# The order of a step's work on TensorE in the attention stage of a fused cross-attention and feed-forward layer, with ScalarE and VectorE made to follow it

## The reference

```python
q = Wq @ layernorm(x) + bq ; k = Wk @ ctx + bk ; v = Wv @ ctx + bv   # per batch, 128x128 @ 128x1024
k, v = pad(k, 8 left, 7 right), pad(v, ...)
dots[h, t, w] = sum_d q[h, d, t] * k[h, d, t + w] * hd ** -0.5
attn = softmax(dots, axis=w)
out[h, d, t] = sum_w attn[h, t, w] * v[h, d, t + w]
x = x + tanh(g_xattn) * (Wo @ out + bo)
x = x + tanh(g_ffn) * ((silu(n @ gate) * (n @ up)) @ down)            # n = layernorm(x)
```

## Time and profile before

| | |
|---|---|
| median of 3 runs | 1725.99 us (1715.70 to 1726.87) |
| the profiled execution | 1736.66 us, its span 1734.8 us |
| PE busy | 1607.8 us, 93% of the span, granted clock 0.96 of full speed in the mean |
| VectorE, ScalarE, GpSimd busy | 1516.9, 995.8, 1455.0 us |
| attention, batches 1 to 14 | 394.04 us (52.88 to 446.92), granted clock 0.91 |

### The profile page before, as it was taken

The page is one execution under the profiler, slowest core; times in us unless marked ns, Lnnn a source line. Parts: engine busy times, 40 slices in busy tenths (PEclk is TensorE's granted clock), DMA queues, the critical chain, the costliest instruction groups (busy, mean ns, idle before and its releaser), DMA issues.

```text
span 1734.8 us, 40469 instructions
## 1 busy us (share of the span) xinstructions
PE 1607.8 (93%) x16614; PEld 823.8 (47%) x16614; DVE 1516.9 (87%) x1482; ACT 995.8 (57%) x1134; POOL 1455.0 (84%) x892
## 2 busy tenths in 40 slices
PE   6888889889658999999999999999999999999996
PEld 4565656566533444444444444444444444444444
DVE  4567667667539999999999999999999999999996
ACT  3566667666534555555555555555555555555552
POOL 4556646565647999999999999999999999999975
PEclk8899989899869999999999999999999999999998
DMA  5645645565333222222222222222222222222127
GB/s 120 154 110 150 140 120 132 128 137 126 96 97 97 74 74 73 73 79 79 75 73 73 75 81 76 73 73 73 74 80 78 73 74 74 78 78 76 37 97 291
DMA packets 162354, 166.66 MB, mean 96 GB/s; under 512 B 11918, under 2 KB 127310, under 8 KB 162154
## 3 DMA queue, kind: packets, MB, share of 16 engines
q1 hardware_dynamic: 161018, 163.74, 33.7%
q10 hardware_dynamic: 1152, 0.33, 0.1%
HBM read 113.92 MB, written 16.78 MB: 75 GB/s over the span
## 4 chain that ended last, share of the span: by engine, by line
PE 81%; issue 6%; POOL 5%; ACT 3%; DMA 1%; DVE 1%; SPq 1%; ACTq 0%; POOLq 0%; DVEq 0%
PE bank L1136 63%; PE bank L1043 3%; POOL oacc L564 3%; PE bank L1032 2%; PE bank L999 2%; PE bank L1075 2%; PE bank L1006 2%; PE bank L991 2%; ACT pT L632 2%; PE bank L1053 1%; ACT xn L639 1%; PE bank L1022 1%; PE bank L995 1%; PE bank L1003 1%; PE bank L1011 1%
## 5 line engine op out<-in xcount | busy, mean ns | idle before, releaser
L924 DVE SCALAR_TENSOR_TENSOR acc<-bank,scale,acc 128x1024 f32<-128x1024 f32 x784 | 949.3, 1271 | 17.7 <-PE bank L1136 10.3
L1136 PE MATMUL bank<-xT,w_int 128*128 128x512 f16 x3584 | 851.3, 381 | 12.0 <-ACT acc L733 4.3
L564 POOL TENSOR_TENSOR oacc<-oacc,d_part 128x1024 f32<-128x1024 f32 x336 | 795.0, 2366 | 26.5 <-ACT d_part L753 10.3
L753 ACT ACTIVATE d_part<-bank,scale 128x1024 f32<-128x1024 f32 x336 | 373.5, 1112 | 390.7 <-PE bank L1136 376.8
L1136 PEld LDWEIGHTS bank<-xT,w_int 128*128 128x128 f16 x3584 | 350.5, 98 | 439.4 <-DVE acc L924 7.1
L1136 PE MATMUL bank<-h_hi,d_int 128*128 128x512 f16 x896 | 340.2, 380 | 7.2 <-ACT d_part L753 3.0
L1136 PE MATMUL bank<-h_lo,d_int 128*128 128x512 f16 x896 | 339.5, 379 | 0.0
L506 POOL TENSOR_TENSOR raw_z<-raw_w,raw_z 128x512 int32<-128x512 int32 x168 | 263.9, 1571 | 29.0 <-DMA raw_z<-in_L_ffn_gate_z_dram 12.2
L632 ACT ACTIVATE pT<-bank 96x1024 f16<-96x1024 f16 x128 | 123.4, 1014 | 61.2 <-PE bank L1043 61.2
L1136 PEld LDWEIGHTS bank<-h_hi,d_int 128*128 128x128 f16 x896 | 87.2, 97 | 150.1 <-DVE acc L924 27.8
L820 DVE TENSOR_REDUCE rmax<-bank 128x16 f32<-128x768 f32 x64 | 60.9, 952 | 104.6 <-PE bank L1032 104.6
(11 more groups left out here) (82 smaller groups left out, 1406.1 us busy)
## 6 DMA issues: line engine op xcount, KB each, us to landing
raw_w<-in_L_ffn_gate_w_dram SPq DMA_DIRECT2D x56, 256.0 KB, 3.0
raw_z<-in_L_ffn_gate_z_dram SPq DMA_DIRECT2D x56, 256.0 KB, 3.7
raw_w<-in_L_ffn_up_w_dram SPq DMA_DIRECT2D x56, 256.0 KB, 3.0
raw_z<-in_L_ffn_up_z_dram SPq DMA_DIRECT2D x56, 256.0 KB, 3.7
raw_w<-in_L_ffn_down_w_dram SPq DMA_DIRECT2D x56, 256.0 KB, 2.7
raw_z<-in_L_ffn_down_z_dram SPq DMA_DIRECT2D x56, 256.0 KB, 3.3
vt<-vn_hl SPq DMA_DIRECT2D x64, 192.0 KB
vt<-vn_hl SPq DMA_DIRECT2D x64, 160.0 KB
```

The source lines that it names most:

```text
L564: nc.gpsimd.tensor_tensor(into, into, part, ALU.add).then_inc(d_added, 1)
L753: nc.scalar.activation(d_part[:, (count(0, x, False) - 1) % 2, :], pair[slot][:, :, :].rearrange("p h r -> p (h r)"), ACT.Copy, scale=scal ...
L924: nc.vector.scalar_tensor_tensor(out=into, in0=pair[u % 4][:, :, :].rearrange("p h r -> p (h r)"), scalar=scale[:, par, i, m, k:k + 1], in ...
L1136: last = nc.tensor.matmul(dst[:, h, :], weights, rows_of(h, part), start=(part == 0), stop=(part == 1))
```

## The change

On PE, two of the three tasks of a step now stand between the scores and the mixing, the third between the mixing and the turning, and none behind the turning. Before, one stood in each place. ScalarE takes the third task before it takes the turned probabilities; VectorE takes the third task in its own step instead of behind the next step's `soften`; and ScalarE's `norm_x(b + 1)` moves from the end of step 0 of batch b to its beginning.

```diff
@@ scalar (ACT)
             for b in range(B):
                 for s in range(S):
                     n = S * b + s
-                    behind_scores, behind_mix, behind_turn = tasks_of(b, s)
-                    for t in behind_scores:
+                    if s == 0 and b + 1 < B:
+                        norm_x(b + 1)
+                    first, second, third = tasks_of(b, s)
+                    for t in first:
                         take_high(*t)
                     exp(n)
-                    for t in behind_mix:
+                    for t in second + third:
                         take_high(*t)
                     if n:
                         take_pT(n - 1)
-                    for t in behind_turn:
-                        take_high(*t)
-                    if s == 0 and b + 1 < B:
-                        norm_x(b + 1)
                     if s == 1 and b >= 2:
                         norm_row(b - 2)
@@ vector (DVE)
                     soften(b, s)
-                    if n:
-                        for t in tasks_of((n - 1) // S, (n - 1) % S)[2]:
-                            take_low(*t)
-                    for t in tasks_of(b, s)[0]:
+                    first, second, third = tasks_of(b, s)
+                    for t in first:
                         take_low(*t)
                     if n >= 2:
                         take_mix(n - 2)
-                    for t in tasks_of(b, s)[1]:
+                    for t in second + third:
                         take_low(*t)
                     if s == 0 and b >= 2:
                         moments_row(b - 2)
@@ vector, behind the loop
             invert_sums(S * B - 3)
             invert_sums(S * B - 2)
-            for t in tasks_of(B - 1, S - 1)[2]:
-                take_low(*t)
             take_mix(S * B - 2)
@@ tensor (PE)
                     scores(b, s)
-                    behind_scores, behind_mix, behind_turn = tasks_of(b, s)
-                    for t in behind_scores:
+                    first, second, third = tasks_of(b, s)
+                    for t in first + second:
                         project(*t)
                     if n >= 2:
                         mix(n - 2)
-                    for t in behind_mix:
+                    for t in third:
                         project(*t)
                     if n == 1:
                         pe.wait_ge(s_kept, 2)
                     if n:
                         turn_probs(n - 1)
-                    for t in behind_turn:
-                        project(*t)
```

## The result

The changed kernel takes 1672.75 us in the median of four runs (1665.99 to 1674.17), the kernel before 1725.11 (1715.70 to 1726.87): a ratio of 0.970, interval 0.966 to 0.974. It is 52 us faster. Forecast were 1702 us and a range of 1687 to 1722: the sign is right, the size is not, and the time lies outside the range on the fast side.

The account below looks back on a forecast made before the run. PE bounds attention: 22.2 us of work in 28.15 a batch, the rest waits and half clock. -21 - 1 + 5 - 4 - 6 = -27 gave 1710, 1699 on the medians' scale; with an allowance 1702 us, range 1687 to 1722.

Parts of the forecast that it names:

- `q` wait removed: Attention batches: PE's 13 waits of the `q` projection for `norm_x` vanish, -14.8 us.
- slow clock that goes with it: Attention batches: PE's slow clock behind four of the longer `q` waits goes too, -6 us.
- new waits for `shifted` and pT: Attention batches: the earlier `norm_x` delays ScalarE and VectorE, so PE waits; +5 us, kept at 2 to 10.
- instruction waits, in the mixings: Mixings of steps 0 and 3: longer instruction packets shorten waits by 0.95 and 0.7 us, seven times each, -11.5 us.
- instruction waits, at the other places: Places where packets get shorter: two of them wait 0.5 us, seven times, +7 us.
- first batch: First batch: one more `q` wait goes and `v` lies before a mixing that waits for a DMA, -1 us.
- last batch: Last batch: earlier emptying of `o(14, 1)` lets SP issue `keep_row(14)` and piece 3's loads 6.1 us earlier, -6 us.
- parts 1 and 3: Earlier `norm_x` in the attention batches, -21, -1 and +5 us; SP's earlier issue in the last batch, -6 us.
- Rival A: Attention batches: instruction delivery takes the `q` wait's place; 1716 us, bounds 1709 to 1722, chance 0.30 shared with another rival.
- Rival B: Attention batches: four shortened packets of every eleven wait and drop the clock; slower, 1750 us, chance 0.09.
- part 2: PE's new task order in the attention batches: same work, instruction waits moved by packet density; -4 us taken.
- Rival C: Attention batches: the stalls in the mixing mostly vanish and nothing new appears; 1684 us, chance 0.11.

Follow-up runs that it names:

- e4: Kernel before with the new order on all engines in the last of the 16 batches only; 1721.33 us, 0.993 of the kernel before.
- e6: Kernel before with 64 additional load and matmul pairs in PE's prologue, shifting packet ends by half a packet; 1726.24 us, 0.999 of the kernel before.
- e12: The changed kernel itself, run again beside other kernels on their chip; 1676.82 us, 0.974 of the kernel before.
- e1: Kernel before with only `norm_x` moved to the head of the batch; 1719.42 us, 0.992 of the kernel before.
- e2: Changed kernel with `norm_x` back at the end of step 0, so only the order is new; 1697.75 us, 0.978 of the kernel before.
- e9: Kernel before with later loads of x and the context cut to 128 of 1024 columns, output not the reference's; 1693.59 us, 0.983 of the kernel before.
- e3: Kernel before with the second task ahead of the mixing, on PE alone; 1714.96 us, 0.989 of the kernel before.
- e11: Kernel before with `norm_x` at the batch's head and the second task ahead of the mixing on PE; 1698.64 us, 0.987 of the kernel before.
- e5: Kernel before with the third task ahead of the turning on all three engines, the second still behind the mixing; 1713.34 us, 0.993 of the kernel before.
- e8: Changed kernel with `take_zero` behind `split_p` in the last batch; 1674.23 us, 0.972 of the kernel before.
- e13: Changed kernel with the second task back behind the mixing on PE; 1693.90 us, 0.982 of the kernel before.
- e15: Changed kernel with the second copy of each batch's values issued after that batch's first scores; 1674.84 us, 0.971 of the kernel before.

## Why the prediction missed, point by point

The order before in three executions (before, e4, e6) has 33.6 us of "issue", 17.8 of `q` wait and 26 of rest in the mean; the changed order in two (changed, e12) has 20.2, 0, and 10. That gives the terms their measured sizes beside the 52 us:

| step of the prediction | forecast | measured |
|---|---|---|
| `q` wait removed | -14.8 | -17.8 |
| slow clock that goes with it | -6 | -2 to -5 |
| new waits for `shifted` and pT | +5 | +0.2 (L1047 for L824); pT none |
| instruction waits, in the mixings | -11.5 | -15 |
| instruction waits, at the other places | +7 | +2 |
| slow clock behind the instruction waits | no term | -11 to -14 |
| first batch | -1 | within scatter |
| last batch | -6 | -4 to -6 |

The slow clock is shared out by e1 and e2. Taking away the `q` wait lowers the rest from 26 to e1's 24 in the order before, and from e2's 15 to 10 in the new order; the new order lowers it from 26 to 15 with the `q` wait there and from 24 to 10 without. The waits for the context's load (L989, one to a trace) are 1.7 and 4.4 us in the changed order, 0, 2.3 and 0 in the order before.

**Right: the mechanisms of parts 1 and 3.** The `q` wait vanished, `norm_x` waits for `shift` (17.1 us in 13 waits) without PE noticing, and the last batch's gain came down SP's queue as laid out. The undisturbed batch takes 22.05 us, where the rows gave 22.2. Rival A, delivery in the wait's place, is refuted by e1: it is 9 to 20 us faster, and "issue" rose by some 5 us of 18, little more than the scatter. Rival B, slower by four short packets, did not occur: the place in steps 1 to 2 went from 4.1 to 3.7 us of window, and its packets come in 3.6.

**The step that failed** is the pricing of part 2, in the words "I take 0.5 for two of them, seven times: +7, and find -4.5" and the "I take -4" behind it. It was worth -13 us in waits, and another -11 to -14 in slow clock, for which the sum had no term. I took the packets' lengths as the whole story and the delivery as given. The runs show a delivery that depends on the data traffic (e9: 30 us less with PE's stream untouched) and that the new order itself changed. At the shortened places it was short enough: +2 us in place of +7.

That the mixings gained about what I had given them, 15 us for 11.5, is partly luck. The packet in step 3's mixing did get a longer window (4.4 to 4.9 us, where I had 0.7 more). The one in step 0's mixing did not: its window went from 5.4 (4.2 in the median) to 4.0 and 4.4 us, where I had 0.95 more, and what shortened its wait was delivery, 7.4 to 4.8 and 6.0.

**The clock was the larger miss.** 29 us of the 14 batches were slow clock by my count (34 by the granted clock) and I attached 6 of them to the waits that would go, and none to speak of to the instruction waits ("-17" with "as much less slow clock" stood among the bounds). Most of it hung on the instruction waits. What made the difference is that these became short, not that they went: 20 and 21 waits. In the kernel before a projection pair behind 0.50 us of waiting took 1.10, and behind 1.58 us 1.74; in the changed kernel 17 of the 21 are below 1 us. In all eighteen traces together, PE lost 1.1 us in the mean to the half clock in the 6 us behind each of 207 waits of 1.5 us or more, and 0.04 us behind each of 316 shorter ones. Of the long ones, `q` waits included, the order before has 19, 16 and 16 (before, e4, e6), the changed one 2 and 7. The same in the timeline, a wait of 0.67 us in step 3's mixing and the pair behind it at full speed:

```profile
92.90 0.44 PE L1069 MATMUL bank<-vt,pT 96*32 96x32 f16 x38 [0.67 <-issue]
93.27 1.13 PE L1000 MATMUL bank<-xn,wo 128*128 128x512 f32 x2
```

**The new waits** were sized for a clean batch that follows a clean one (5.9 us for step 1; batch 4 shows 5.88). Every second batch follows an instruction wait in step 3, and then `shift` comes only 0.4 to 0.7 us behind the scores and step 1 takes 5.50. Fourteen times 0.5 should have been at most seven times.

Rival C ("more is won", 1684) came nearest in what happened and got a chance of 0.11, though the stalls in the mixing did not vanish but halved (28 to 13 us), and the time came out 11 us below it. With the clock counted at its full share something like it would have been the forecast: 14.8 + 11.5 + most of 29 + 6 is 55 to 60 us.

**What the places do.** The traces, read by place, say why both tasks had to move. At step 0's mixing the third task's place moves the packet's request (instruction 256 k + 160) against the loads of x and the context: it comes 3.7 to 5.3 us behind the issue of the context's load where the third is behind the turning (before, e1, e3, e4, e11), and the packet's DMA starts 3.5 to 5.1 us later; where the third is ahead (e2, e5, e8, e13 and both executions of the changed kernel) it comes 6.1 to 6.9 us behind, and the DMA starts 2.2 to 3.2 us later. These are means of seven packets each. The second task's place sets the window: 3.3 us in the median in e5 and 3.4 in e13, 4.0 to 4.3 in e2 and the changed kernel; at step 3's mixing it is 4.5 where the second is behind the mixing and 4.9 to 5.0 where it is ahead. So e5 and e13 have the earlier packet with the shorter window, e3 and e11 the longer window with the late packet. This is read from the traces afterwards; no run moved the loads alone in time.

**What stays open.** At step 3's mixing the delivery is 5.8 us in e5 against 6.8, at the same window, and 5.3 in e1, which did not touch the order on PE; with 8 us of "issue" between executions of one kernel, part of such differences may be scatter, which was not tested. Why e15's later second copy gained nothing, and what e3's 19 us are, is open too.

## What to carry to other kernels

Where a trace shows engine waits without a releaser in an unrolled kernel, count instructions against the packets of the engine's instruction queue: they tell which stretch of code is too dense for its fetch. What helped here was a task between two dense groups, a later request behind the loads, and less DMA traffic. Price a wait together with the slow clock that follows it: bringing the mixing's waits from some 2.0 us down to 0.9 and 1.2 gave back about as much again in clock. Check that the window of a count is the window of the length it is held against: one wait at its edge was 3 us here. And take a term's size from more than one execution where waits of this kind scatter; the one profiled here was 0.6% above its median.

## What the runs showed of the hardware

- Every wait of PE on "issue" over 0.4 us in the 14 batches of three traces (53 waits; 307 of 309 in all eighteen) began at instruction 256 k + 449 and ended about 1.5 us after instruction packet k had landed. A packet (16 KB) takes 0.9 to 1.4 us by itself in 70 of 77 cases; what varies is when it starts, 0.2 to 6.9 us behind instruction 256 k + 160 in the attention stage of the kernel before.
- Data DMAs delay instruction packets: some 0.8 MB a batch less data (51.50 MB in the 14 batches before, 40.33 in e9) took "issue" from 32 to 36 us down to 12. "Runtime: NRT & Kernel Launch" of the Trainium skill, Instruction fetch mechanics, calls the fetch hidden; for this kernel it is not, with 7 to 39 us of such waits in the 14 batches, and the traces decide.
- PE's granted clock in the 14 batches was 0.91 in the kernel before, with 33 waits of which 19 were 1.5 to 3.2 us long, and 0.99 in the changed one, which has two such waits (1.7 and 1.9 us) among 23.
